# Token attention: values projected in the fourth turn, and the centre of the input computed by GpSimd

## The reference

```
qkv = x @ qkv_w.T                      # x is the normalised input; 16 heads of 8
raw = q @ k.T                          # per head, 256 x 256
scores = alpha * tanh(raw / beta) + lam * hamming + lat   # last two bilinear in tanh(x @ small)
attn = softmax(where(causal, scores, -inf))
out = (attn @ v) @ out_w.T
```

## Time and profile before

| | us |
|---|---|
| median of 3 runs | 4054.79 |
| lowest, highest | 4053.88, 4055.74 |
| the profiled execution | 4051.72 |
| its span | 4049.9 |

### The profile page before, as it was taken

How to read it: one execution, slowest core, us unless ns; L and a number is a source line. 1 busy time by engine, 2 the same in 40 slices (tenths; PEclk the granted TensorE clock), 3 DMA queues, 4 the chain that set the end, 5 groups by cost and what they waited for, 6 DMA issues and landing times. The chain is left out here.

```text
span 4049.9 us, 104259 instructions
## 1 busy us (share of the span) xinstructions
PE 3822.8 (94%) x34969; PEld 2917.7 (72%) x34969; DVE 2984.6 (74%) x7049; ACT 2676.5 (66%) x6409; POOL 1939.4 (48%) x1865
## 2 busy tenths in 40 slices
PE   7999999969999989899999889999999999999999
PEld 5666666647777766577777557777777777789998
DVE  6888888869999965799998665555555555566666
ACT  7888888857778853678787336666666666633333
POOL 4666666657777731566666333334333333311111
PEclk9999999979999999999999999999999999999999
DMA  3000000000000001000000110000000000000000
GB/s 105 1 0 0 0 0 0 0 14 20 20 24 20 24 22 27 14 13 16 13 16 18 24 34 2 1 0 0 0 0 0 0 0 0 0 6 9 9 9 9
DMA packets 69052, 47.65 MB, mean 12 GB/s; under 512 B 38360, under 2 KB 57952, under 8 KB 68832
## 3 DMA queue, kind: packets, MB, share of 16 engines
q1 hardware_dynamic: 68960, 46.43, 4.4%
HBM read 12.62 MB, written 4.19 MB: 4 GB/s over the span
## 5 line engine op out<-in xcount | busy, mean ns | idle before, releaser
L1672 ACT ACTIVATE l_probs<-l_act,l_neg_max 128x128 f32<-128x128 f32 (+1 forms) x1024 | 415.5, 425 | 274.0 <-DVE l_neg_max L1629 271.4
L1609 POOL TENSOR_TENSOR l_probs<-l_probs,l_sums 128x512 f32<-128x512 f32 x384 | 391.0, 1039 | 366.1 <-DVE l_sums L1637 366.1
L400 POOL TENSOR_TENSOR t_probs<-t_probs,t_neg_max 128x512 f32<-128x512 f32 x384 | 390.9, 1039 | 298.6 <-DVE t_neg_max L469 298.4
L1629 DVE TENSOR_REDUCE l_neg_max<-l_act 128x2 f32<-128x512 f32 (+1 forms) x384 | 246.9, 684 | 356.3 <-PE l_act L1728 356.3
L1990 ACT ACTIVATE e_hT<-e_act 128x512 f32<-128x512 f32 x256 | 152.8, 597 | 285.3 <-PE e_act L2011 285.3
L459 DVE SCALAR_TENSOR_TENSOR t_probs<-t_tanh_qk,scalars_sb,t_dve 128x512 f32<-128x512 f32 x384 | 269.4, 743 | 83.6 <-ACT t_tanh_qk L569 52.9
L854 POOL TENSOR_TENSOR w_swappedQ<-w_rawQ,w_table 128x512 f32<-128x512 f32 x128 | 162.1, 1289 | 261.1 <-ACT w_rawQ L1071 261.1
L569 ACT ACTIVATE t_tanh_qk<-t_act,t_inv_beta 128x512 f32<-128x512 f32 x384 | 246.5, 707 | 57.9 <-PE t_act L636 57.7
L2023 PEld LDWEIGHTS e_dve<-e_sb,e_hT 128*128 128x128 f32 x2048 | 268.7, 191 | 13.3 <-ACT e_hT L1990 0.2
L854 POOL TENSOR_TENSOR w_swappedK<-w_rawK,w_table 128x512 f32<-128x512 f32 x128 | 228.6, 1807 | 93.0 <-ACT w_rawK L1071 93.0
L2023 PE MATMUL e_dve<-e_sb,e_hT 128*128 128x128 f32 x2048 | 269.8, 275 | 0.0
(11 more groups left out here) (260 smaller groups left out, 10533.0 us busy)
## 6 DMA issues: line engine op xcount, KB each, us to landing
w_v_mid<-w_v SPq DMA_DIRECT2D x128, 130.0 KB, 2.3
z<-w_z_copy SPq DMA_DIRECT2D x32, 128.0 KB, 2.0
h<-z SPq DMA_DIRECT2D x32, 128.0 KB
out<-x_sb SPq DMA_DIRECT2D x32, 128.0 KB, 1.8
h<-z SPq DMA_DIRECT2D x32, 127.0 KB
wqkv_sb<-L_ffn_wqkv SPq DMA_DIRECT2D x2, 768.0 KB, 6.8
kv_up_sb<-L_attn_w_kv_up SPq DMA_DIRECT2D x1, 1024.0 KB, 9.4
e_sb<-L_ffn_w SPq DMA_DIRECT2D x1, 1024.0 KB, 5.6
```

The source lines that it names most:

```text
L400: nc.gpsimd.tensor_tensor(p, p, neg_max[:, j, 0:len(gs)].unsqueeze(2) .broadcast_to((P, len(gs), P * (t + 1))), ALU.add).then_inc(shifted. ...
L1609: nc.gpsimd.tensor_tensor(p, p, sums[:, at, 0:len(hs)].unsqueeze(2) .broadcast_to((P, len(hs), P * (t + 1))), ALU.mult).then_inc(divided.s ...
L1629: nc.vector.tensor_reduce(neg_max[:, units.index(name), 0:len(hs)], to_act.bank("s" + name, back)[:, :].rearrange("p (h j) -> p h j", h=le ...
L1672: ins = nc.scalar.activation(probs[:, at % SLOTS, s * width:(s + 1) * width], bank[:, s * width:(s + 1) * width], ACT.Exp, bias=neg_max[:, ...
```

## The change

The value projection of `front` goes from turn 4 to turn 3. On TensorE it stands between the transposes of `o0` and `o1`, on ScalarE behind the exponentials of turn 3 and ahead of the normalised input. The centre goes from one operation of VectorE in turn 2 to two of GpSimd behind its reciprocal root: 0 - mean, then times rstd. It has a semaphore of its own, and a tile of zeros is set at the start.

```diff
--- before.py
+++ after.py
@@ -267,9 +267,9 @@
 
     VALUES, LATE_VALUES = {5: "yT0"}, {2: "yT1"}
     DIVIDE, BACK, OUT = 3, 4, 5
-    MOMENTS, CENTER, SCALE = 1, 2, 3
+    MOMENTS, SCALE = 1, 3
     ahead_at = {4: ["xnT"], 5: ["right"]}
-    front_at = {0: ["left", "q"], 1: ["k"], 4: ["v"]}
+    front_at, amid = {0: ["left", "q"], 1: ["k"]}, {DIVIDE: "v"}
 
     act_order, dve_order = [], []
     for i in range(turns):
@@ -279,7 +279,7 @@
         act_order.append("pT" + units[2 * (i - LAG)])
         act_order += ["oT"] if i == BACK else []
         dve_order.append("pT" + units[2 * (i - LAG) + 1])
-        act_order += ahead_at.get(i, []) + front_at.get(i, [])
+        act_order += ahead_at.get(i, []) + front_at.get(i, []) + ([amid[i]] if i in amid else [])
         act_order += ["out"] if i == BACK else []
         dve_order += ["o0", "o1"] if i == DIVIDE else []
 
@@ -324,12 +324,13 @@
         oT = sb("oT", [P, T])
         y = sb("y", [P, TILES, D])
         center = sb("center", [P, TILES])
+        zero = sb("zero", [P, TILES])
         act_banks = [ctx.enter_context(nc.psum_tensor(f"t_act{i}", [P, BANK], F32)) for i in range(RING)]
         dve_banks = [ctx.enter_context(nc.psum_tensor(f"t_dve{i}", [P, BANK], F32)) for i in range(RING)]
 
         ahead_jobs = [job for jobs in ahead_at.values() for job in jobs]
         late_jobs = ["pT" + name for name in late(LAG)] + ["yT1", "o0", "o1", "oT", "out"]
-        front_jobs = [job for jobs in front_at.values() for job in jobs]
+        front_jobs = [job for jobs in front_at.values() for job in jobs] + list(amid.values())
         back_jobs = [job for job in act_order + dve_order if job not in ahead_jobs + late_jobs + front_jobs]
 
         def ring(banks, name, order):
@@ -341,10 +342,11 @@
         shifted = Count(sem("shifted"), units, [], units)
         exped = Count(sem("exped"), in_turns(EXP), [], units[:2 * (turns - EXP)], late(EXP))
         den = Count(sem("den"), ["o0", "o1"], [], [], ["o0", "o1"])
-        pre = PRE_NORM[:4] + ["center"]
+        pre = PRE_NORM[:4]
         post = POST_NORM[:4]
         vec = Count(sem("vec"), pre + post, pre, [], post)
         updated = Count(sem("updated"), ["ydiff", "yn", "x"], [], [], ["ydiff", "yn", "x"])
+        centred = Count(sem("centred"), ["minus", "center"], ["minus", "center"])
         scaled = Count(sem("scaled"), ["xn0", "xn1"], ["xn0", "xn1"])
         rst = Count(sem("rst"), RSQRT, RSQRT[:2], [], RSQRT[2:])
         norm = Norm(nc, ctx, "t_", vec, rst, c)
@@ -366,7 +368,8 @@
 
                 for u in range(2):
                     nc.gpsimd.memset(v[u][:, :, :, :], 0.0).then_inc(setup_pool, 1)
-                pool.wait_ge(setup_pool, 3)
+                nc.gpsimd.memset(zero[:, :], 0.0).then_inc(setup_pool, 1)
+                pool.wait_ge(setup_pool, 4)
                 for u in range(2):
                     nc.gpsimd.memset(v[u][:, :, :, TD:TD + 1], 1.0).then_inc(setup_pool, 1)
 
@@ -389,6 +392,12 @@
                     for i in range(turns):
                         if ahead and i == MOMENTS + 1:
                             norm.rsqrt(pool, "", ahead)
+                            nc.gpsimd.tensor_tensor(center[:, :], zero[:, :], norm.mv[""][:, :, 0], ALU.subtract)\
+                                .then_inc(centred.sem, 1)
+                            pool.wait_ge(rst.sem, rst.done("rstd", ahead))
+                            pool.wait_ge(centred.sem, centred.done("minus", ahead))
+                            nc.gpsimd.tensor_tensor(center[:, :], center[:, :], norm.rstd[""][:, :], ALU.mult)\
+                                .then_inc(centred.sem, 1)
                         if done and i == OUT:
                             norm.rsqrt(pool, "y", done)
                         for name in twins(i) if back else []:
@@ -505,11 +514,6 @@
 
                                 dve.wait_ge(scaled.sem, scaled.done("xn1", ahead.before()))
                             norm.pre_moments(dve, ahead, x)
-                        if ahead and i == CENTER:
-                            dve.wait_ge(rst.sem, rst.done("rstd", ahead))
-                            nc.vector.scalar_tensor_tensor(center[:, :], norm.mv[""][:, :, 0], -1.0,
-                                                           norm.rstd[""][:, :], ALU.mult, ALU.mult)\
-                                .then_inc(vec.sem, 1)
                         for t in range(TILES if done and i == DIVIDE else 0):
                             divide(t, done)
 
@@ -588,8 +592,10 @@
                         for jobs, seq in ((ahead_at, ahead), (front_at, front)):
                             for job in jobs.get(i, []) if seq else []:
                                 projected(job, seq)
+                        if front and i in amid:
+                            projected(amid[i], front)
                         if ahead and i == SCALE:
-                            act.wait_ge(vec.sem, vec.done("center", ahead))
+                            act.wait_ge(centred.sem, centred.done("center", ahead))
                             for t in range(TILES):
                                 nc.scalar.activation(norm.xn[:, t], ahead.tile(x, t), ACT.Identity,
                                                      scale=norm.rstd[""][:, t:t + 1], bias=center[:, t:t + 1])\
@@ -614,7 +620,7 @@
                                            w["basis"][:, b, :], twT[:, :], start=True, stop=True)
                 ins.then_inc(setup_pe, 1)
                 pe.wait_ge(setup_dve, 11)
-                pe.wait_ge(setup_pool, 5)
+                pe.wait_ge(setup_pool, 6)
 
                 def rows(n):
 
@@ -699,6 +705,14 @@
                                                    bilinear[:, j].rearrange("a n s b -> a (n s b)"),
                                                    bits[u][0:2 * BITS, 0, :], start=True, stop=True)
                     ins.then_inc(to_act.filled.sem, 1)
+
+                def quotients(t, done):
+                    to_dve.wait_free(pe, f"o{t}", done)
+                    to_act.wait_drained(pe, "yT1", done)
+                    for n in range(GROUPS):
+                        ins = nc.tensor.transpose(to_dve.bank(f"o{t}", done)[:, n * P:(n + 1) * P],
+                                                  yT[:, n, t * P:(t + 1) * P], c["ident"][:, :])
+                    ins.then_inc(to_dve.filled.sem, 1)
 
                 def step(ahead, front, back, done):
                     for i in range(turns):
@@ -730,13 +744,11 @@
                                                        oT[:, t * P:(t + 1) * P], w["t_out"][:, :],
                                                        start=True, stop=True)
                             ins.then_inc(to_act.filled.sem, 1)
-                        for t in range(TILES if done and i == DIVIDE else 0):
-                            to_dve.wait_free(pe, f"o{t}", done)
-                            to_act.wait_drained(pe, "yT1", done)
-                            for n in range(GROUPS):
-                                ins = nc.tensor.transpose(to_dve.bank(f"o{t}", done)[:, n * P:(n + 1) * P],
-                                                          yT[:, n, t * P:(t + 1) * P], c["ident"][:, :])
-                            ins.then_inc(to_dve.filled.sem, 1)
+                        for t in range(TILES if i == DIVIDE else 0):
+                            if done:
+                                quotients(t, done)
+                            if front and t == 0:
+                                project(amid[i], front)
 
                 pipeline(pe, n_seq, step, 4)
```

## The result

| | before | after |
|---|---|---|
| median, us | 4054.34 (4 runs) | 4017.81 (4 runs) |
| lowest, highest | 4047.74, 4055.74 | 4016.33, 4021.03 |
| span of the profiled execution | 4049.9 | 4015.0 |
| one steady step of the token attention | 25.18 | 23.97 |

The ratio after to before is 0.992, 95% interval 0.9906 to 0.9934: faster by 0.8%. The forecast was 4015 with a range of 4008 to 4032. The steps are read as the distance between the starts of t_rstd on GpSimd, over 24 of them.

A forecast was written before the change was run, and what follows sets the result against it. A chain from engine to engine, no full engine, bounds the step. 0.49 + 0.84 = 1.33 us over 30 steps is 39.9, taking the profiled 4051.7 to 4011.8; with 3.1 for the median, 4015 us, range 4008 to 4032.

The forecast's parts named there:

- The loop: Turns 4 and 5: TensorE's scores wait for VectorE's t_pT and ScalarE's t_xnT on a closing chain; step 25.17 us.
- The centre: VectorE's sum of turn 3 starts sooner without the centre ahead of it: 0.49 us a step, bounds 0.47 and 0.55.
- The values: Projection hidden in turn 3; scores of turn 5 stop waiting for xnT's copy and start 0.84 us sooner, or 0.68.
- The sum: Token attention: 0.49 + 0.84 = 1.33 us a step, 25.17 to 23.84; 39.9 us over 30 steps.
- (a): Centre's gain lost: L459 inherits the GpSimd wait or ScalarE's tanh becomes the bound; 25 us gained, 4030, chance 0.10.
- (b): Start of turn 5 does not move, another of its waits ending just behind xnT; 15 us gained, 4040, chance 0.06.
- (c): No effect: both gains are given back in turns 5 to 2; 4055 us, chance 0.04.
- (d): Slower: GpSimd's pair before turn 2's additions delays turn 4's tanh, gain gone from 2.6 us; 4075 us, chance 0.05.

The follow-up runs named there:

- the repeat: The unmodified changed kernel run again with a second trace, beside the kernel before (4050.7 us): 4012.9 us, ratio 0.9906, step 23.96 us.

## Why the prediction was right

**The loop.** It named the waits at turns 4 and 5 as the places that set the step. The table of distances shows it: over all nine kernels of the table only these two columns move, the other four stay within 0.01 us. Engine busy times would not have told this.

**The centre.** 0.49 was predicted and 0.48 measured, alone and together with the rest. The price was the distance from its start to the next operation, not its own length or the 160 ns that it takes alone, and the reason given (a GpSimd instruction under way) was shown by moving it. The sum L459 did not inherit the wait: its pair takes 1.41 beside GpSimd. That the number fits so well is in part luck. The centre started 0.08 before the end of the maxima, and a sum that did the same would have gained 0.55, the upper bound. The prediction put it 0.06 later than that, for no reason that its rows give, and in the run those 0.06 are a wait for ScalarE's first tanh, which it had taken as ready in time.

**The values.** Hidden on TensorE and ScalarE in turn 3, as worked out: o1 has no new delay that counts, and ScalarE keeps 0.16 of cover. The gain in turn 5 was put at 0.84 and is 0.74. The step that was mis-sized is what follows the output projection: I took 0.55 from its start to the scores, by the spacing of its own matmuls, and it is 0.64. The first scores matmul comes 0.20 us after the last matmul of the output projection, whose own spacing is 0.11. That the transition costs more than the spacing could be read in the earlier trace rows, where the four have a length of 0.71; the prediction had 0.68 as its lower bound from this, and the truth lies between.

**The sum.** 1.21 a step instead of 1.33. The profiled executions lie 34.9 us apart, by the sum it should have been 39.9. From three landmarks in the traces (t_rstd of steps 4 and 31, the last copy t_y): up to step 4 the kernel after is 1.5 us behind, from there to step 31 it gains 32.6 (27 times 1.21), to the end of the block another 4.2, and the rest of the program gives 0.5 back. The 1.5 behind in the first steps goes with TensorE's later start at full clock; the repeat is 1.1 ahead there and has a span of 4012.0. The end of the block is partly clock again. In these windows of the block's last 24 us (columns: length, busy PE, PEld, DVE, ACT, POOL, granted clock) the granted clock is 0.67 before and 0.88 after, and the last eight transposes of output tiles take 1.94 and 1.07 us:

```profile
821.00:845.00 24.00, 13.95 (x171) 10.38 (x169) 8.68 (x26) 7.92 (x15) 9.69 (x14) 0.67 0.01 2
```

```profile
786.00:810.00 24.00, 12.69 (x188) 9.66 (x184) 11.29 (x33) 10.44 (x20) 11.37 (x20) 0.88 0.01 2
```

What the first step lost by the two operations on GpSimd is 0.3, as predicted (t_xn starts at 14.97 instead of 14.66). The medians lie 36.5 apart, thirty times 1.21 is 36.3; with some us of clock on either side of it, and a forecast that took the runs shown as 3.1 above the profiled one, where they are 0.9 above it in the result, the closeness of 4017.8 to 4015 is partly luck.

**The rivals.** (a) and (b) would each have kept one column of the table unchanged; both moved. (c) would have needed a third column to grow; none did. (d) works as described, with the pair at 0.47 us and its break-even, by estimate, at 2.6. Its price of 1.6 us for one operation was misread, though. That L875 takes 0.71 on its first execution, at 848.42, with VectorE idle; from 863.96 on it takes 1.65 and more, and there it starts just behind VectorE's two-input multiplication L1034 (863.83, 1.23). It is mostly a wait for VectorE. Beside the new pair VectorE runs the copy L508 and the maxima L478, each with one input.

## What to carry to other kernels

Price an operation by what follows it on the chain that closes, not by its duration: a 128x2 operation cost 0.5 us because it waited for another engine's instruction, and moving it one place took nearly all of that away. Then look for what holds the follower next (here the tanh): it caps the gain. In a ring of buffers a job has two costs, its work and the place that it takes in the order; after any move list for each filling job which drain stands in front of it, since a wait for a copy late in another engine's queue costs more than the job's own work. And read the cover that remains by doubling what uses it: the missing idle mark in a timeline does not say that it is gone.

## What the runs showed of the hardware

- A VectorE operation with both inputs in SBUF waits until a GpSimd addition or multiplication of 128x512 under way ends: 151 ns for 128x2 with GpSimd idle, 626 beside its additions; 174 to 176 ns for 128x16 with GpSimd idle, up to 1198 beside its multiplications. Inside GpSimd's power of 128x16 (2.89 us) it does not wait: 174 ns.
- The other way round, GpSimd's power of 128x2 takes 0.71 us alone and 1.65 to 1.78 when it starts just behind a two-input VectorE operation of 1.22 us.
- GpSimd subtractions and multiplications of 128x2 are cheap here: 0.20 each, ten without waits in 1.55 us; with a semaphore wait between two, 0.27 from start to start.
- Two traces of one program differ in when TensorE reaches its upper clock level in the first 40 us (four matmuls of 256 columns in 2.07 and in 1.13 us). In the first steps alone this moves a span by 2 to 3 us, where by its steps one of the two edits gives 14 or 22 in all. Small differences want the steady step, not the span.
